# 16-head attention: the mask by rows of queries over half of the columns, and the low value of the unwritten places written once

## The reference, cut to what matters

```
logits = einsum('bhqd,bhkd->bhqk', q, k) * scale + incidence * weights * bias_scale
logits = where(diffs < 0, -inf, logits)          # diffs = query position - key position
attn = softmax(logits)                           # 8 batches x 16 heads, 512 x 512
out = einsum('bhqk,bhkd->bqhd', attn, v) @ w_out.T + b_out
```

## Time and profile before

| | us |
|---|---|
| median of three timed runs | 1046.6 (1043.72 to 1048.62) |
| the profiled execution, its own time | 1043.87 |
| the profiled execution, its span | 1042.6 |

### The profile page before, as it was taken

The page is one execution under the profiler, slowest core; times in us unless marked ns, Lnnn a source line. Parts: engine busy times, 40 slices in busy tenths (PEclk is TensorE's granted clock), DMA queues, the critical chain, the costliest instruction groups (busy, mean ns, idle before and its releaser), DMA issues.

```text
span 1042.6 us, 25479 instructions
## 1 busy us (share of the span) xinstructions
PE 867.4 (83%) x9999; PEld 529.3 (51%) x9999; DVE 746.9 (72%) x1784; ACT 657.5 (63%) x1154; POOL 406.3 (39%) x664
## 2 busy tenths in 40 slices
PE   5688888876465798998989899898978868898987
PEld 2344455554343465665656566565555533444434
DVE  4776888898585778677786877868878547666554
ACT  4668888746133365756566575665656747685866
POOL 3043455456865544373553645444232210101000
PEclk8899999998766699999999999999999989999999
DMA  5000000000324262543425334261552000000000
GB/s 148 22 1 1 1 1 1 1 1 3 103 65 117 67 169 50 127 122 88 130 66 138 81 98 120 66 171 47 133 145 65 3 1 1 21 2 21 1 22 21
DMA packets 70698, 63.60 MB, mean 61 GB/s; under 512 B 30600, under 2 KB 62824, under 8 KB 70576
## 3 DMA queue, kind: packets, MB, share of 16 engines
q1 hardware_dynamic: 70064, 61.90, 22.1%
q10 hardware_dynamic: 512, 0.02, 0.0%
HBM read 34.02 MB, written 27.36 MB: 59 GB/s over the span
## 4 chain that ended last, share of the span: by engine, by line
PE 45%; DVE 11%; issue 6%; ACT 5%; POOL 2%; DVEq 0%; POOLq 0%; ACTq 0%
PE bank L2081 12%; PE bank L1662 7%; PE bank L1637 3%; PE bank L1610 3%; PE bank L1602 3%; PE bank L1618 3%; PE bank L1599 2%; PE bank L1592 2%; DVE bank L1745 1%; ACT 4g L2139 1%; PE bank L1628 1%; DVE 4f L2175 1%; PE bank L1670 1%; PE bank L1625 1%; DVE roots L1299 1%
## 5 line engine op out<-in xcount | busy, mean ns | idle before, releaser
L1823 ACT ACTIVATE ET<-bank 64x512 f32<-64x512 f32 x128 | 75.5, 590 | 102.3 <-PE bank L1628 101.5
L2162 DVE TENSOR_TENSOR act<-4f,act 128x512 f16<-128x512 f32 x96 | 66.4, 691 | 57.7 <-ACT act L2129 57.5
L1818 ACT ACTIVATE ET<-bank 128x768 f32<-128x768 f32 x128 | 103.2, 806 | 2.3
L1745 DVE TENSOR_TENSOR bank<-bank,W 128x256 f32<-128x256 f32 x128 | 54.7, 427 | 51.6 <-PE bank L1592 51.6
L1750 DVE TENSOR_TENSOR bank<-bank,WT 128x256 f32<-128x256 f32 x128 | 55.3, 432 | 49.9 <-PE bank L1618 49.9
L1755 DVE TENSOR_REDUCE mo<-bank 128x4 f32<-128x512 f32 x128 | 87.8, 686 | 2.7 <-PE bank L1602 2.5
L1662 PE MATMUL bank<-ET,vv 128*32 128x128 f32 (+2 forms) x1792 | 89.1, 323 | 0.8 <-DVE O L1780 0.8
L2129 ACT ACTIVATE act<-4f 128x512 f16<-128x512 f32 x96 | 60.4, 630 | 28.6 <-DVE 4f L2175 26.6
L1763 DVE TENSOR_REDUCE mo<-bank 128x3 f32<-128x384 f32 x128 | 70.0, 547 | 0.0
L1764 DVE TENSOR_REDUCE mo<-bank 128x3 f32<-128x384 f32 x128 | 70.0, 547 | 0.0
L1602 PE MATMUL bank<-maskq,identh 128*64 128x512 bf16 x256 | 62.7, 396 | 0.0
(11 more groups left out here) (377 smaller groups left out, 2539.7 us busy)
## 6 DMA issues: line engine op xcount, KB each, us to landing
ring<-scr_q SPq DMA_DIRECT2D x16, 324.0 KB
QO<-scr_q SPq DMA_DIRECT2D x16, 324.0 KB
ring<-scr_a SPq DMA_DIRECT2D x16, 252.0 KB
KA<-scr_a SPq DMA_DIRECT2D x16, 252.0 KB
ring<-scr_k SPq DMA_DIRECT2D x16, 168.0 KB
KB<-scr_k SPq DMA_DIRECT2D x16, 168.0 KB
scr_a<-dk SPq DMA_DIRECT2D x8, 288.0 KB, 2.6
X<-in_x SPq DMA_DIRECT2D x8, 256.0 KB, 4.9
```

What stands on the lines that cost most here:

```text
L1745: dve.tensor_tensor(half(psD, 1), half(psD, 1), over(W[:, h * HB:(h + 1) * HB], NT), ALU.mult).then_inc(s_wq, 1)
L1818: act.activation(ET[n % NE][:, T:SEG * P], psXT[:, 0:NP * P], ACT.Exp).then_inc(s_expo, 1)
L1823: act.activation(to[0:HB, :], psDT[0:HB, :], ACT.Exp)
L2162: dve.tensor_tensor(lo, f32_[f % 3], hi, ALU.subtract).then_inc(s_lo, 1)
```

## The change

The table `maskq` loses its first 64 columns, and with them the two memsets that fill them. The mask of L1602 is now added over `half(psD[z, :], 1)` only, 256 columns for each half of the query rows instead of 512. Of the places that it no longer covers, the upper query half got 0 from it; the lower query half, first key half, which no product writes, gets -1e30 by one memset on DVE at the beginning of the stage. PE waits for that memset (`s_place`) before the first head's incidences.

```diff
-    s_w, s_wb, s_edge = c.signals("3", "w wb edge")
+    s_w, s_wb, s_edge, s_place = c.signals("3", "w wb edge place")
...
-    maskq, maskk = sb("maskq", P, dt=BF16), sb("maskk", HB, dt=BF16)
+    maskq, maskk = sb("maskq", HB, dt=BF16), sb("maskk", HB, dt=BF16)
...
     def clamp_dve():
-        dve.memset(maskq[0:HB, 0:HB], -1e30)
-        dve.memset(maskq[HB:P, 0:HB], 0.0)
         dve.wait_ge(s_lg, 32)
...
-            dve.tensor_copy(maskq[z, HB:P], sh.maskh[z, z])
+            dve.tensor_copy(maskq[z, :], sh.maskh[z, z])
...
                 for z in HALVES:
-                    m = pe.matmul(tiles(psD[z, :]), sh.identh[:, z], over(maskq, NT), start=False, stop=True, skip_group_check=True)
+                    m = pe.matmul(half(psD[z, :], 1), sh.identh[:, z], over(maskq, NT), start=False, stop=True, skip_group_check=True)
                 m.then_inc(s_own, 1)
...
             side = ahead.pe
+            pe.wait_ge(s_place, 1)
             incidences(0)
...
+            dve.memset(half(psD[0:HB, :], 0), -1e30).then_inc(s_place, 1)
             for x in ET:
                 v = dve.memset(half(x[HB:P, 0:T], 0), 0.0)
```

## The result

The changed kernel takes 1035.57 us (median of six runs, 1030.92 to 1036.43), the kernel before 1044.7 (six runs, 1041.84 to 1048.62). The ratio is 0.9895, with a 95% interval from 0.9869 to 0.9920: about 1.05% faster. Run again beside others it was 1034.36 (four runs), ratio 0.9878, interval 0.9848 to 0.9908. The forecast was 1034.5. The two medians by themselves are 9.1 us apart (a ratio of 0.991); the ratio of 0.9895 stands for 11.0 us, the two profiled spans for 10.4.

What follows compares the result with a forecast made beforehand. PE's order of work was taken to set the pace, though not alone. 98 pairs x 0.107 plus 5 cold x 0.21, less 0.2 and 0.27, gave 11.1 us; forecast 1034.5 us, range 1030 to 1043.

Steps and rivals of the forecast that it cites:

- The price of a pair: Mask matmuls on PE: 256 columns fewer bring the next weight load 0.107 us earlier per head at 2.4 GHz.
- rival C: Columns are not the price of a mask pair; only the memset is left, no change, 1046.9 us; chance 0.08.
- The count of paying heads in a steady batch: Steady batches of sixteen heads: 15 masks on the chain, one more head per batch struck because ACT releases its L1618.
- The head with 0.07 us of room: One head per batch, where L1745 ends just before PE's L1599: saves 0.04 us less, 0.2 us over six batches.
- The count over the whole stage: Attention stage, 326 to 845 us: 109 mask pairs on the chain, less 6, so 103 paying, five of them cold.
- Rival A: Steady batches: time saved becomes PE's waits for DVE, 5 us left, 1041 us; chance 0.17.
- The cold heads: Stage's start before 356 us, at the half clock: 5 pairs worth 0.21 us each, 1.05 us.
- The memset: New PSUM memset on DVE opening the stage, on the chain: costs 0.27 us.
- The last batch: L1299 at 710.19 us to the last `weigh`: few masks count between the fetch wait and 791 us; 2.35 us gained.
- rival B: Granted clock drops to 0.50 somewhere between 356 and 814 us; 35 us of it makes 1052 us; chance 0.05.
- clock 1.00 from about 356 us to the stage's end: Expected sign in the attention stage: PE's granted clock stays at the 2.4 GHz level after the first eight heads.
- The end: From the last `weigh` to the end of the span: predicted gain 0.

Runs made afterwards that it cites:

- half_at_12_13: The kernel before with the 256-column mask only in heads n mod 16 = 12 and 13; a steady batch took 62.84 us, against 63.05.
- two_of_256: The kernel before with each 512-column mask matmul issued as two of 256 columns; a steady batch took 63.09 us.
- after_again: The changed kernel itself, run and profiled again; 1034.36 us, ratio 0.9878 to the kernel before.
- before_act: The kernel before with ACT, not SP, issuing the DMA of the maxima row; last L1299 to last `weigh` 99.27 us, against 102.24.
- place_only: The kernel before plus the new memset and PE's wait, mask left at 512 columns; a steady batch took 63.05 us, first memset to first `weigh` 2.49.
- half_at kernels: The kernel before with the 256-column mask only in heads n mod 16 = 8 and 9, or 12 and 13; a steady batch took 63.035 or 62.84 us.
- cols_128: The changed kernel with the mask over the first two tiles only, 128 columns a half; a steady batch took 60.89 us.
- after_act: The changed kernel with ACT, not SP, issuing the DMA of the maxima row; 1034.92 us, ratio 0.9886.
- moved_act: The changed kernel with the eight ET memsets moved to heads 3 and 4 and ACT issuing the maxima row's DMA; 1030.31 us, ratio 0.9855.

## Why the prediction was right

- *The price of a pair.* 0.107 us, read from L1628: right. The load distance fell from 0.40 to 0.30 us and half_at_12_13 gave 0.21 us for two. That the columns and not the matmuls make it is shown by two_of_256 (rival C is out).
- *The count of paying heads in a steady batch.* 14 x 0.107 less 0.04 is 1.46; measured 1.51. The chain alone would have said 15 (1.6). Of the two heads without room one gains 0.00, the other 0.03 us. The head with 0.07 us of room gained 0.09: it lost 0.02, not 0.04.
- *The count over the whole stage* was wrong. The chain holds 101 mask pairs from 326 to 845 us, not 109: seven of the eight views name L1602 once more in their line of shares, and the pair at 380 us stands in two of them. Five are cold, six lie ahead of L1299 of the second batch, 75 in the five steady batches and 15 behind L1299 at 710.19. With 101 the prediction's own sum is 10.2 us, not 11.1. The cold heads and the five batches keep their terms.
- *Rival A* is refuted for the steady batches: the six DVE waits kept their 5.1 us, and fourteen heads kept what they saved.
- *The cold heads.* 1.60 of 1.7 us in the profiled run, and partly luck. By head 8 the changed kernel is 1.03 us ahead of the kernel before, and after_again 1.04, as 5 x 0.21 says. Then after_again loses 1.3 us between heads 9 and 11: its half clock ends 36.9 us after the first `weigh`, the changed kernel's first profile's 31.7 us after it.
- *The memset.* 0.38 us instead of 0.27: the row of the SBUF memsets gave the duration, not the gap behind this one.
- *The last batch* is the term that was mis-sized. "Few masks count until 791 us" still left 22 paying heads in my sum, 2.35 us; with 15 in the chain and one less for head 9 it would have been 1.5. The runs show what else the term lacked: nothing of the gain gets past the fetch for certain, because the wait for it varies by more than the gain, and where the fetch is out of the way (the chain of before_act has 21 pairs there) the cut saves 1.66 us by head 123 and a fall of the clock takes back 1.0.
- *The clock* (rival B) did fall, at 749.5 and at 783.6 us, 3.4 us each time; my statement "clock 1.00 from about 356 us to the stage's end" was wrong. The first fall, behind the wait for the fetch, is not the change's doing: place_only and two_of_256, with the long mask, fell there for 6.8 us and both half_at kernels for 3.4, and with the wait gone no kernel fell there. The second fall is another matter. It comes between 782 and 793 us right behind a wait of PE for L1744 of 1.5 to 1.7 us, in five of the six profiles with the 256-column mask in every head (not in after_again, nor in cols_128) and in none of the six others with the long mask in all or fourteen of sixteen heads, where these waits are mostly some 0.1 us shorter (1.40 to 1.55 us). The same split stands at the stage's start: the half clock ends 28.7 to 30.3 us after the first `weigh` in those six, and 36.7 to 36.9 us after it in five of the seven with a shorter mask. That looks like a small part of rival B. It cost 0.8 to 1.3 us each time, and with some 9 us more at the half clock in all it stays below the 22 that would eat the gain. It is not settled: each kernel has one profile, and over the timed runs the mean granted clock is the same, 0.943 in ten of the changed kernel and in eighteen of the kernel before.
- *The end.* I had given nothing to the last stage, and it became 2.05 us shorter. The same instructions run there (1402 matmuls in both windows). In the thirteen profiles it takes 228.1 to 231.7 us, in the order of the time it spends at the half clock, with few exceptions: 10.2 us in those of 228.1 to 228.6, 13.7 at 229.1, 25.7 at 231.7. In the sum of 10.4 us this stroke of luck stands against the missing 2.9 of the last batch. The total came out closer than its terms deserved: after_again, the same kernel, lies 7.0 us below the kernel before by its profiled span.

## What to carry to other kernels

Price a matmul that is cut by the start of the next weight load in a timeline, beside a pair of the same form that the kernel already has, and not by its duration or its busy time. Count the places that pay on the chain of what ended last, then strike those where a second chain ends within less than the saving. In a loop with a fixed period both can be checked to 0.01 us with one profile, where the whole times here spread over half a percent and more. Compare the two profiles head by head and not by their sums: a steady gain per head and a loss all at once have different causes. And look for the one wait that is longer in the last round of a loop: 1.13 us saved ahead of it were 0.22 behind it, and kept where the transfer started earlier.

## What the hardware showed that I had not expected

- A memset of 64x256 f32 in PSUM and one in SBUF have the same row, 0.27 us, but behind the one in PSUM the next memset started 0.11 us after the row's end (326.13 + 0.27 and 326.51; the same in place_only, after_again and after_act). Whether PSUM, the signal or the other partitions of the next memset make it is open.
- DVE, ACT and POOL are busy for the same time in a steady batch of the changed loop within 0.07 us from profile to profile (DVE 47.16 to 47.20). What differs between runs of one kernel is TensorE's clock: how long it stays low at the stage's start (the changed kernel was at the half clock for 34.1 us from 326.2 on, the same kernel run again for 47.8 from 320.4 on), whether it falls after a wait, and how often in the last stage. Each microsecond at 1.2 GHz in the last stage cost some 0.23 us: (231.68 - 228.12)/(25.7 - 10.2).
- ACT issued a DMA whose row lasts 0.75 us (740.67 in moved_act) while its exponential of 0.79 us, started at 740.54, ran on. The next activation, at 742.34, waited for PE and not for the issue, and a steady batch stayed at 61.55 us.
